# Moving most of the preparation of an edge loop into its early half steps

## The reference

```python
h = x @ W_in + b_in
Wij = (ssp(f_ij @ Wf1 + bf1) @ Wf2 + bf2) * rcut_ij[:, None]      # 20 numbers an edge
agg = segment_sum(h[dst] * Wij, src)              # sums at src from rows at dst
x = layernorm(x + ssp(agg @ Wo1 + bo1) @ Wo2 + bo2)
# second layer: attention over the same edges, its weights a softmax over the edges of a node
x = layernorm(x + gnn_attention(x, src, dst))
```

## Time and profile before

| | |
|---|---|
| median of 3 runs | 1388.13 us (1387.0 to 1388.74) |
| profiled execution | 1386.31 us, its span 1384.5 us |
| busy: PE, DVE, ACT, POOL | 1156.9, 1199.6, 856.2, 813.5 us |
| share of the span | 84%, 87%, 62%, 59% |
| mean granted clock of TensorE | 0.928 of full speed |

### The profile page before, as it was taken

The page is one execution under the profiler, slowest core; times in us unless marked ns, Lnnn a source line. Parts: engine busy times, 40 slices in busy tenths (PEclk is TensorE's granted clock), DMA queues, the critical chain, the costliest instruction groups (busy, mean ns, idle before and its releaser), DMA issues. The chain is left out here.

```text
span 1384.5 us, 27852 instructions
## 1 busy us (share of the span) xinstructions
PE 1156.9 (84%) x8980; PEld 940.2 (68%) x9072; DVE 1199.6 (87%) x2226; ACT 856.2 (62%) x2125; POOL 813.5 (59%) x905
## 2 busy tenths in 40 slices
PE   5786776799989868899979999999999495877895
PEld 4453454457778646788757887777777484877895
DVE  8798876649999869899879999999998579999986
ACT  2564575577878878788878888888876054000023
POOL 3377777777777777777777777777777320000011
PEclk9697898799999999999999999999999797889998
DMA  8232242266998477899698998998898883766661
GB/s 258 80 92 83 82 131 81 75 160 173 241 271 235 150 249 219 236 245 253 207 238 222 271 261 256 241 260 231 241 268 226 210 254 116 237 207 231 226 218 38
DMA packets 246566, 276.09 MB, mean 199 GB/s; under 512 B 35079, under 2 KB 194470, under 8 KB 243078
## 3 DMA queue, kind: packets, MB, share of 16 engines
q1 hardware_dynamic: 197762, 183.84, 45.1%
q0 software_dynamic: 25792, 53.29, 12.2%
q10 hardware_dynamic: 22852, 37.02, 11.9%
HBM read 162.85 MB, written 111.20 MB: 198 GB/s over the span
## 5 line engine op out<-in xcount | busy, mean ns | idle before, releaser
L1977 POOL DMA_INDIRECT edge_rows<-x_rows,pos x806 | 779.6, 967 | 252.8 <-issue 229.5
L1475 ACT ACTIVATE h_edge<-ps_wh,w_col 128x128 f32<-128x128 f32 x808 | 229.3, 367 | 105.4 <-PE ps_wh L1276 100.3
L1320 PEld LDWEIGHTS ps_d<-back_one,back 128*128 128x128 f32 x1914 | 231.6, 193 | 60.9 <-issue 57.2
L1320 PE MATMUL ps_d<-back_one,back 128*128 128x128 f32 x1914 | 240.7, 278 | 5.1 <-DVE agg_t L1794 4.6
L1283 PE MATMUL ps_wh<-wf,filt 128*128 128x128 f32 x1616 | 236.6, 292 | 0.8 <-DVE filt L1577 0.7
L1269 PE MATMUL ps_v<-f_t,wf 128*128 128x512 f32 x400 | 222.4, 639 | 0.0
L1581 DVE TENSOR_TENSOR x_rows<-ps_wh,h_edge 128x512 f32<-128x512 f32 x202 | 138.2, 684 | 89.8 <-DMA edge_rows<-x_rows,pos 50.1
L1283 PEld LDWEIGHTS ps_wh<-wf,filt 128*128 128x128 f32 x1616 | 207.3, 201 | 2.8 <-DVE filt L1577 2.8
L1112 PE MATMUL ps_wh<-yard 128*128 128x150 bf16 x1575 | 138.4, 233 | 59.8 <-DVE yard L1102 37.4
L2434 PE MATMUL ps_wh<-loan,yard 128*126 128x129 f32 x1250 | 155.9, 289 | 37.8 <-DVE yard L2692 29.9
L1112 PEld LDWEIGHTS ps_wh<-yard 128*128 128x128 bf16 x1575 | 109.0, 100 | 105.0 <-DVE yard L1102 81.2
(11 more groups left out here) (344 smaller groups left out, 1368.2 us busy)
## 6 DMA issues: line engine op xcount, KB each, us to landing
c_tab<-yard SPq DMA_DIRECT2D x25, 1575.0 KB
yard<-c_tab SPq DMA_DIRECT2D x25, 1575.0 KB, 6.6
dst_bc<-dst ACTq DMA_DIRECT2D x99, 252.0 KB
back<-edge_rows SPq DMA_DIRECT2D x42, 516.0 KB
edge_rows<-x_rows,pos POOLq DMA_INDIRECT x806
back<-edge_rows SPq DMA_DIRECT2D x48, 258.0 KB
m_tab<-yard SPq DMA_DIRECT2D x25, 393.8 KB
mask_room<-m_tab SPq DMA_DIRECT2D x5, 1968.8 KB, 12.7
```

The costliest lines, as they stand in the source:

```text
L1320: mm = nc.tensor.matmul(acc(c), back_rows(n)[:, k0 + t, 0:D], back_one[:, m % 2, o + t, :], start=t == 0, stop=t == k1 - k0 - 1, skip_grou ...
L1475: copy = nc.scalar.activation(h_edge[:, j, q, :], ps_wh[:, bank, 1, q * D:(q + 1) * D], ACT.Copy, scale=w_col[:, t(q)])
L1977: return pool.indirect_dma_start(table[s], bass.IndirectOffsetOnAxis(places_here, 0), rows, None)
```

## The change

The preparation ranks the first 256 tiles only (TA), and of those it finishes the first 32: their places are made before the loop. It makes the first 640 rows of h (chunk 0). The rest stands in a new function `settle(k)` of TensorE, ScalarE and VectorE, called once in each half step:

- VectorE: the first numbers of tiles 32 to 167 and the window and row numbers of the far tiles (256 to 807) at half step 0; one ranked part in each of the half steps 1 to 5; the 25 masks of the far tiles in four parts at 1 to 4; five chunks of 512 rows of h, a step of each in a half step from 2 to 16; counts, turned counts, scans, bases, first numbers of the far tiles at 7, 9, 10, 12, 13; totals at 16 and 18, constants at 20. The other 38 ranked parts stand at three a half step from 14 on (RANK_REST).
- Tables go from half step 10 to 28, ranges from 24 to 30 (17 of the steps one a half step, with two doubled), pairs from 41 to 46 (still every second half step), counting from 51..190 to 54..196. One of the two banks of the ranges and pairs is now the spare bank ps_wh[:, 1, 1], so that pairs and sets can stand together. Sets before half step 54 read their numbers from SBUF.
- SP loads x in two pieces, loads 11 constants in group 1, stores the chunks of h at groups 3 to 9 and the zeros at groups 11 to 14, from a source of one row. The first 12 groups must find their window in the first 640 rows; the count of windows takes that in.
- GpSimd makes no remainders of h any more and does not fill f_t; ScalarE fills f_t, and agg_t at half step 20.

The diff, cut:

```diff
+TA = 2 * P
+LB = 4
+NL = (NB - CB) // LB
+NCH = 1 + NL
+NEAR_ROWS = CN
+NEAR = 12
+RANK_REST = 14
...
             @block.vector
...
-                rank_link(nc.vector.tensor_scalar(hi_i[:], src_col[:], 7, None, ALU.logical_shift_right))
-                rank_link(nc.vector.tensor_copy(hi_bf[:], hi_i[:]))
-                for w in range(NB):
-                    ins = nc.vector.tensor_scalar(win1[:, w, :], hi_bf[:], float(w), None, ALU.is_equal)
-                rank_link(ins)
+                rank_link(nc.vector.tensor_scalar(lo_i[:, near], src_col[:, near], 7, None, ALU.logical_shift_right))
+                rank_link(nc.vector.tensor_copy(hi_bf[:, near], lo_i[:, near]))
+                rank_link(window_masks(0, NB, near))
...
                 for k in range(OBS[0]):
                     dve.wait_ge(own_mm, k + 1)
                     own_picked(0, k, ps_all[k]).then_inc(own_done, 1)
-                first_sums(RB[1], NT)
-                first_parts(RB[1], NT)
-                dve.wait_ge(rank_mm, 5)
-                rank_link(nc.vector.tensor_copy(tot_all[:], ps_d[:, 0, 256:256 + NS * NB]))
-                assert ranked[0] == RK_PREP
+                dve.wait_ge(own_done, OBS[0])
+                own_place(0).then_inc(own_sum, 1)
+                dve.wait_ge(own_sum, 1)
+                place(0).then_inc(pos_put, 1)
...
-            RANK_FROM = 1
-            TABLES_AT = 10
+            RANKS_END = RANK_REST + -(-(len(RANKED) - OBS[1]) // 3)
+            TABLES_AT = RANKS_END + 1
             RK_ALL = RK_PREP + 8
-            R_FROM = 24
-            P_FROM = R_FROM + 17
-            C_FROM = P_FROM + 10
-            C_LAST = NH - 12
+            R_FROM = (RANKS_END + 2) // 2 * 2 + 2
+            P_FROM = R_FROM + 16
+            C_FROM = P_FROM + 8
+            C_LAST = NH - 6
...
             def ranked_at(k):
-                return range(max(0, k - RANK_FROM) * 2, min(len(RANKED), max(0, k - RANK_FROM + 1) * 2))
+                if k < RANK_REST:
+                    return range(k - 1, k) if 1 <= k <= OBS[1] else range(0)
+                first = OBS[1] + 3 * (k - RANK_REST)
+                return range(min(len(RANKED), first), min(len(RANKED), first + 3))
+            def masks_at(k):
+                return (NB * (k - 1) // 4, NB * k // 4) if 1 <= k <= 4 else None
+            def chunk_at(k, later):
+                n = k - later
+                return n // 3 + 1 if n >= 0 and n % 3 == 0 and n // 3 < NL else None
...
             @block.sync
...
+                        if i == 1:
+                            load_constants()
+                        for c in range(1, NCH):
+                            if i == (3 * c + 2) // 2 + 1:
+                                store_rows(sp, c, h3_of(c))
+                        if 11 <= i < 11 + NS // 2:
+                            store_zeros(range(2 * (i - 11), 2 * (i - 10)))
                         if 2 * i == R_FROM - 2:
                             load_edges()
+                        if i + 2 == NEAR:
+                            all_written()
...
             @block.tensor
...
                 def rank_product(n):
-                    if n >= 2:
-                        pe.wait_ge(own_done, OBS[0] + n - 1)
+                    if n == 0:
+                        pe.wait_ge(rk, RK_NEAR)
+                    if n == OBS[1]:
+                        pe.wait_ge(rk, RK_FIRST)
+                    pe.wait_ge(own_done, OBS[0] + max(0, n - 1))
                     b, k = RANKED[n]
                     own_product(b, k, ps_d[:, n % 2, :]).then_inc(own_mm, 1)
+                def settle(k):
+                    for n in ranked_at(k):
+                        rank_product(n)
+                    if chunk_at(k, 1) is not None:
+                        h_part(chunk_at(k, 1))
+                    if k == 5:
+                        counts_part(range(TA // P, 5))
...
             @block.scalar
...
+                def settle(k):
+                    if chunk_at(k, 2) is not None:
+                        high_h(chunk_at(k, 2))
+                    if chunk_at(k, 3) is not None:
+                        middle_h(chunk_at(k, 3))
...
             @block.vector
...
+                def settle(k):
+                    if k == 0:
+                        ranked[0] = 11
+                        near_firsts()
+                        far_numbers()
+                    for n in ranked_at(k):
+                        rank_part(n)
+                    if masks_at(k) is not None:
+                        ins = window_masks(*masks_at(k), far)
...
+                    if chunk_at(k, 2) is not None:
+                        rows_h(chunk_at(k, 2))
+                    if chunk_at(k, 3) is not None:
+                        rest_h(chunk_at(k, 3))
+                    if chunk_at(k, 4) is not None:
+                        last_h(chunk_at(k, 4))
+                    if k == 7:
+                        far_counts()
+                    if k == 9:
+                        far_rows()
+                        segment_scan(1)
+                        segment_scan(2)
...
+                    if k == 12:
+                        far_bases()
...
-                        for n in ranked_at(k):
-                            rank_part(n)
+                        settle(k)
                         if k == TABLES_AT:
                             rest_of_tables()
+                        if k in SET_AT:
+                            back_ones(SET_AT[k], iota_ps if k >= C_FROM else iota_f[:])
```

More of the change, by code:

```diff
@@ L274, in plot @@
                 rows, count = shape[0], math.prod(shape[1:])
[L275 to L278, removed]
+                taken = -(-count * size // 4)
+                flat = room[0:rows, at[0]:at[0] + taken]
+                at[0] += taken
+                assert at[0] <= words
                 if dt is not F32:
@@ L421, in place, with rank_counts @@
             return nc.vector.tensor_copy(pos[:, t0:t0 + n], pos_f[:, 0:n])
+        row = lambda ap: ap.rearrange("(a n) -> a n", a=1)
+        col = lambda ap: ap.rearrange("(n a) -> n a", a=1)
+        tri25 = before_w[:, :, :].rearrange("p a b -> p (a b)")[:, 0:R2]
+        spare_bank = ps_wh[:, 1, 1, :]
+        def rank_counts(b, at, ones_here):
+            t0, n = tiles_of(b)
+            for w in range(NB):
+                mm = nc.tensor.matmul(at[0:n, w:w + 1], win1[:, w, t0:t0 + n], ones_here, start=True, stop=True)
+            return mm
@@ new lines, in rank_turn, with window_masks, segment_scan @@
+        def rank_turn(b):
+            t0, n = tiles_of(b)
+            return nc.tensor.matmul(ps_d_flat[0:R2, t0:t0 + n], tile_n[0:n, b, :], ident[0:n, 0:n], is_transpose=True)
+        def window_masks(w0, w1, t):
+            for w in range(w0, w1):
+                ins = nc.vector.tensor_scalar(win1[:, w, t], hi_bf[:, t], float(w), None, ALU.is_equal)
+            return ins
+        def segment_scan(s):
+            t = slice(SEG[s], SEG[s + 1])
+            return nc.vector.tensor_tensor_scan(run_n[:, t], tile_nt[:, t], tile_nt[:, t], 0.0, ALU.add, ALU.max)
@@ L1190, in more_windows @@
                         sp.wait_ge(win_in[j], 16)
+                    load_constants()
+                    for c in range(1, NCH):
+                        store_rows(sp, c, h3_of(c))
+                    all_written()
+                    store_zeros(range(NS))
                     load_edges()
@@ L1396, in more_windows @@
                 def more_windows():
-                    for n in range(len(RANKED)):
-                        rank_product(n)
+                    for k in range(RANKS_END):
+                        settle(k)
                     count_all()
@@ L1540, in more_windows @@
                 def more_windows():
-                    act.wait_ge(lo_made, 2)
+                    for k in range(RANKS_END):
+                        settle(k)
+                    act.wait_ge(lo_made, 4)
                     count_all()
@@ new lines, in totals, with spread @@
+                def totals():
+                    dve.wait_ge(rank_mm, 7)
+                    nc.vector.tensor_copy(bases_f[:], spare_bank[0:1, 0:NS * NB])
+                    nc.vector.tensor_copy(bases[:], spare_bank[0:1, 0:NS * NB])
+                    rank_link(nc.vector.tensor_copy(tot_row[:], spare_bank[0:1, 256:256 + NS * NB]))
+                    assert ranked[0] == RK_TOT
+                def spread():
+                    dve.wait_ge(rank_mm, 8)
+                    rank_link(nc.vector.tensor_copy(tot_all[:], spare_bank[:, 0:NS * NB]))
+                    assert ranked[0] == RK_PREP
```

668 lines of the change are left out of this document (373 added, 295 removed).

## The result

The changed kernel takes 1393.73 us (median of 7 runs, 1391.51 to 1394.53), the kernel before 1387.0 beside it: ratio 1.0045, interval 1.0033 to 1.0056. It is slower, where 1378.4 and a range up to 1389 were forecast. The profiled execution took 1391.51 us, its span is 1389.7.

A forecast was written before the change was run, and what follows sets the result against it. GpSimd's scatter queue was taken as the bound. 25.7 us gained at the start, less 13, 1.5 and 1.5, made 9.7 us less: 1376.6 for the profiled execution, 1378.4 as median; whole range 1364 to 1389.

The forecast's parts named there:

- What bounds the kernel, and the start: Whole loop: GpSimd's scatter queue bounds, 1.262 us each; shorter VectorE preparation brings the first scatter 25.7 us earlier, to 33.9.
- Rival 3: Preparation ends with SP, destinations still landing at 15 us: 4 us less gain, 1382.4 us; chance 0.14.
- Half steps 0 to 13: Loop start with work moved from preparation: GpSimd does not wait; VectorE's margin at half step 14 is 7.3 us.
- Half steps 14 to 26: Three ranked parts each: VectorE needs 89 us, GpSimd 65.65; GpSimd waits 16 us, 13 net lost.
- I add 0.6 to 0.9: Half steps 14 to 26: cost of the third ranked part on VectorE, giving 4.15 us a half step.
- rival 2: Half steps 14 to 26: TensorE at its lower level between reductions, 5.6 us each; 1397 us, slower; chance 0.13.
- the 3.39 us: Kernel before, half steps 4 to 21: VectorE's time a half step with two ranked parts, waits included, without reductions and tables.
- Tables, ranges: Tables at half step 28 take 5.7 us without margin; half step 27 gives it back; margin grows again from 30.
- Counting to 196: Late loop: counting runs six half steps longer, carrying 1.23 groups each; 1.5 us lost (0 to 4).
- Pairs and sets: Half steps 50 to 53: pairs meet sets, with numbers read from SBUF; 1.5 us lost (0 to 3).
- The rule beside the row: Before half step 14: scans and masks beside scatters could block GpSimd up to 13 us; adds nothing to the sum.

The follow-up runs named there:

- the control: Changed kernel with only totals and constants moved to half steps 26 to 29, no added matmuls: 1389.17 us, ratio 0.9996 to the kernel before.
- third bank: Changed kernel with ranked parts rotating over three PSUM banks from half step 15, totals and constants moved to 27 to 30: 1378.38 us, ratio 0.9928 to before.

## Why the prediction was wrong

- *What bounds the kernel, and the start*: right. The loop begins 25.74 us earlier (25.7 said), the masks take 3.48 us (3.4), the scatter comes at 33.25 (33.9). Rival 3 did not happen: VectorE ends the preparation, not SP.
- *Half steps 0 to 13*: right in kind. GpSimd waits 1.2 us, 1.0 of it at half step 1, and the margin at 14 is 11.6 us (7.3 said, 3 to 11): the woven work was 2 us cheaper, and GpSimd lost 2.8 us itself.
- *Half steps 14 to 26*: this step failed, in the wait that a third part brings, which the sum put at next to nothing. "I add 0.6 to 0.9" gave 4.15 us a half step. Of the 94.5 us for twelve, 29 are five reductions with their casts and 3.8 other moved steps; the rest, 61.7, is 5.1 us a half step. That is past the 4.9 from which rival 2 was said to decide. The stretch of the kernel before from which the 3.39 us came, half steps 4 to 21, as a window and in VectorE's waits for parts and for the filter:

```profile
75.34:167.65 92.31, 69.78 (x427) 42.04 (x432) 81.25 (x136) 51.85 (x136) 68.81 (x72) 0.83 0.31 89
...
DVE yard L410 <- PE ps_d L402: 7.1, 8, 1.9
...
DVE x_rows L1581 <- PE ps_wh L1283: 0.7, 2, 0.5
```

  VectorE's busy time a half step, without reductions, tables and moved steps, was 2.7 us there (81.25 less 29 and 5.7, over 17) and is 3.3 in the changed kernel (73.0 less 29 and 3.8, over 12): the work of one more part, and about all that the added 0.6 to 0.9 pays for. Its idle time was 0.65 us a half step and is 1.8. The 1.1 us that were left out are half the wait for parts (0.9 instead of 0.4 us a half step) and half the wait of the product for the filter (0.6 instead of 0.04), because gather and filter of the next half step stand behind the waiting product in TensorE's list (1.3 to 2.9 us at a time). GpSimd's waits in half steps 14 to 29, beyond the usual 0.30, came to 23.0 us instead of 16 (1.8 in the kernel before), with 4 us more margin than said. A second term was missing: totals and constants were priced as VectorE's work alone, and with their place ahead of TensorE's gathers they made 5.8 of these 23 us (the control). Rival 2 named the two banks but put the loss down to TensorE's lower level; the runs show the banks as the cause of 8.5 us of it (third bank against control) and leave open what the level adds.
- *Tables, ranges*: as said, the margin comes back after half step 27.
- *Counting to 196*: "I take 1.5" is too small. The late waits grew by 3.9 us and the rest behind the last scatter by 2.8; ending at 190 takes back 2.9 and 2.0. The second part was not in the sum, which had "What follows the last scatter is not touched": VectorE's last sums end after the last scatter and the block ends with them.
- *Pairs and sets*: 1.5 us said; not found. Scatters of over 1.1 us cost half steps 14 to 29 and 30 to 60 3.4 and 2.1 us before, and 0 and 5.4 after: the 3.4 us more that the table has in 30 to 60 are nearly all moved there, with the ranges.
- *The switch of code at half step 101*: not in the sum at all. Before, it was hidden behind 8.6 us of margin; in the changed kernel it took 3.4 us longer, met 7.6 us of margin and cost 3.4.
- *The rule beside the row*: its sum held. Seven scans and the masks made GpSimd's scatters in half steps 0 to 13 only 1.2 us longer than before, not 13.

The differences add up (before rounding): 26.4 less at the start; 1.2 + 17.6 + 3.4 + 3.4 more in the first half of the loop and 3.9 - 0.8 in the second; 2.8 behind it; 0.1 elsewhere: 5.2 us more, the difference of the spans.

## What to carry to other kernels

When work is packed more densely on two engines that hand buffers to each other, count the buffers: with one more step in a round than there are banks, the producer waits for the consumer, and the price is not that wait alone but also all that stands behind it in the producer's list; here the two were equal parts. An earlier start is worth only what the queue that follows keeps; read the margin of the bounding queue half step by half step, also at places that cost nothing now (a switch of code, the last sums), because these come out when the margin is spent. Here the same move of the preparation costs 0.45% with three parts a half step on two banks; it gives 0.7% with three on three, 1.0% with two on two, and 1.3 to 1.4% with three banks when counting ends at 190 and the switch stands at 90 as well.

## What was not expected of the hardware

With two parts a half step the sets from half step 50 on read their numbers from SBUF for ten half steps instead of four, and scatters that began inside these compares were stretched. Beside such compares scatters took 3.6 us more than usual in half steps 30 to 60, and 0.4 in the changed kernel. VectorE and GpSimd in order of time, two parts a half step:

```profile
331.00 0.81 DVE L1685 TENSOR_TENSOR back_one<-back_lo,iota_f 128x640 f32<-128x640 f32 x1
331.06 1.59 POOL L2188 DMA_INDIRECT edge_rows<-x_rows,pos  x1 [0.30 <-issue]
```

and a compare with its numbers in PSUM, in the changed kernel:

```profile
616.21 1.09 DVE L1685 TENSOR_TENSOR back_one<-back_lo,ps_d 128x896 f32<-128x896 f32 x1
616.43 0.96 POOL L2188 DMA_INDIRECT edge_rows<-x_rows,pos  x1 [0.31 <-DVE x_rows L1657]
```

Of the scatters that began with over 0.5 us of such a compare ahead of them, the 4 against SBUF numbers took 1.34 to 1.75 us, 1.52 on average, the 36 against PSUM numbers 0.96 at most (two parts a half step). In all fourteen profiles together, the 14 that began 0.06 us or more after a compare against SBUF numbers took 1.34 to 1.77 us; one that began 0.03 us after it took 0.95 (counting to 190). Of 305 that began 0.06 us or more after a compare against PSUM numbers none took over 0.98. With the numbers in PSUM the scatter runs beside the compare; with both inputs in SBUF it is longer, in each of the 14, by what was left of the compare less 0.12 or 0.13 us. The Trainium skill, SBUF — State Buffer, section Who interferes with whom, says that an instruction of VectorE with two SBUF inputs contends with one of GpSimd that reads SBUF, and one with a single SBUF input, outside the modes that use both ports, does not; these rows agree with it in both cases.
